# A prototype-matching block with a quantised FFN: VectorE's short operations rewritten, and the call orders of four engines changed

## The reference, cut to what matters

```python
xn = (x - mean_c(x)) / sqrt(var_c(x) + 1e-6)           # over the 96 channels
y[v, j] = <xn_j, w_mask_v> / (|xn_j| |w_mask_v|)       # cosine with 512 prototypes
v, j = argmax(y); top = y[v, j]; sims = y[v, :]        # of all 512 x 9
mix = concat(xn_j * top + w_mask_v * (1 - top), sims)  # 96 + 9
vcs = tanh(W_i2 leaky_relu(W_i1 mix + b, 0.2) + b)
h2  = W_l2 relu(W_l1 vcs + b) + b                      # 288 = 32 x 9
t   = x + fold(W_conv h2)                              # residual
n   = (t - mean_c(t)) / sqrt(var_c(t) + 1e-5)
out = t + q(W2 q(relu(q(W1 q(n)) + b1)) + b2)          # q: fp8 e5m2 / fp16 grid
```

## Time and profile before

| | |
|---|---|
| median of 3 runs | 2237.98 us (2236.76 to 2238.84) |
| the profiled execution | 2232.82 us |
| its span, first to last instruction | 2231.0 us |
| mean granted TensorE clock | 0.975 |

### The profile page before, as it was taken

One profiled execution on the slowest core, in us unless ns is written; L12 is line 12 of the kernel. 1 busy time (PEld: TensorE's weight loads), 2 busy tenths in 40 slices (PEclk: granted clock), 3 DMA queues, 4 the chain that ended last, 5 costly groups with the idle time before them and its releaser, 6 DMA issues.

```text
span 2231.0 us, 47761 instructions
## 1 busy us (share of the span) xinstructions
PE 2007.8 (90%) x13105; PEld 1485.3 (67%) x13105; DVE 2111.6 (95%) x7422; ACT 1834.2 (82%) x5381; POOL 1548.6 (69%) x1041
## 2 busy tenths in 40 slices
PE   5889999999999999999999999999999999999865
PEld 4566766667666676666766667676666766767653
DVE  7889999999999999999999999999999999999952
ACT  1158888888888888888888888888888888888886
POOL 2467677777767767677676777767777677777742
PEclk9899999999999999999999999999999999999975
DMA  3212323222232232322323232232322323223101
GB/s 98 76 58 81 99 82 107 81 91 96 87 101 82 90 97 85 103 81 91 97 84 104 82 97 92 89 98 82 105 83 89 99 81 99 89 89 98 42 37 48
DMA packets 65481, 193.34 MB, mean 87 GB/s; under 512 B 13688, under 2 KB 15938, under 8 KB 65218
## 3 DMA queue, kind: packets, MB, share of 16 engines
q1 hardware_dynamic: 52866, 170.80, 23.8%
q0 software_dynamic: 10240, 18.89, 2.9%
q10 hardware_dynamic: 2112, 0.60, 0.1%
HBM read 133.23 MB, written 57.02 MB: 85 GB/s over the span
## 4 chain that ended last, share of the span: by engine, by line
DVE 42%; PE 23%; POOL 22%; issue 11%; ACT 2%; POOLq 1%; DMA 0%; ACTq 0%; DVEq 0%
DVE best_y L1031 14%; POOL xl L400 6%; DVE stats L1040 5%; PE bank L701 5%; POOL prod L379 5%; POOL o_pm L391 4%; POOL t_dev L368 4%; DVE h L1048 4%; PE y_ps L646 3%; POOL tq L356 3%; PE y_ps L648 3%; PE y_ps L647 3%; DVE top_v L1070 2%; DVE w_index L1077 2%; DVE t_pm L1056 2%
## 5 line engine op out<-in xcount | busy, mean ns | idle before, releaser
L1031 DVE TENSOR_REDUCE best_y<-y_ps 128x2 f32<-128x1024 f32 (+1 forms) x640 | 698.0, 1107 | 17.5 <-PE y_ps L648 14.6
L463 ACT CAST y<-bank 128x384 f16<-128x384 f32 x1152 | 554.1, 481 | 72.8 <-PE bank L671 68.4
L646 PE MATMUL y_ps<-proto_hi,xh 96*128 96x512 f32 x1152 | 573.4, 498 | 43.6 <-DVE best_y L1031 16.1
L356 POOL TENSOR_TENSOR tq<-t_dev,ra 128x864 fp8e5<-128x864 f32 x128 | 209.4, 1636 | 537.8 <-DVE ra L1012 537.8
L671 PE MATMUL bank<-tqt,f_w 96*128 96x384 f16 x1152 | 392.6, 341 | 141.6 <-ACT y L463 110.4
L472 ACT ACTIVATE h<-h 128x1152 fp8e5<-128x1152 f16 x384 | 448.8, 1169 | 68.3 <-DVE h L1048 68.2
L647 PE MATMUL y_ps<-proto_lo,xh 96*128 96x512 f32 x1152 | 460.4, 400 | 0.0
L648 PE MATMUL y_ps<-proto_hi,xl 96*128 96x512 f32 x1152 | 459.6, 399 | 0.0
L671 PEld LDWEIGHTS bank<-tqt,f_w 96*128 96x128 f16 x1152 | 111.6, 97 | 382.2 <-ACT y L463 266.6
L400 POOL TENSOR_TENSOR xl<-xc,xh 96x1152 fp32r<-96x1152 f32 x128 | 336.9, 2632 | 26.5 <-ACT xh L533 15.8
L1048 DVE TENSOR_SCALAR h<-y,f_b 128x1152 f16<-128x1152 f16 x384 | 306.9, 801 | 22.5 <-ACT y L463 22.5
(11 more groups left out here) (133 smaller groups left out, 4115.9 us busy)
## 6 DMA issues: line engine op xcount, KB each, us to landing
xc<-x_cm SPq DMA_DIRECT2D x128, 432.0 KB, 3.9
xp<-x_pm SPq DMA_DIRECT2D x128, 432.0 KB, 4.6
out<-o_pm SPq DMA_DIRECT2D x128, 432.0 KB, 2.4
xsel<-x_pm,x_index POOLq DMA_INDIRECT x128, 2.5
wsel<-proto_rows,w_index POOLq DMA_INDIRECT x128, 4.7
proto_rows<-proto SPq DMA_DIRECT2D x1, 384.0 KB, 2.7
proto<-w_mask SPq DMA_DIRECT2D x1, 192.0 KB, 3.7
f_f<-w_1t ACTq DMA_DIRECT2D x1, 144.0 KB
```

Of the source, the lines that this page charges most:

```text
L463: act.copy(y16[:, q, r, 0:TOK], bank[0][:, 0:TOK]).then_inc(s_y16, 1)
L646: pe.matmul(y, hi, proto_hi[:], start=True, stop=False)
L1031: dve.tensor_reduce(best_y[t % 2][:, j0:j1], y_ps[n % 2][:, 0:j1 - j0, :], AX_X, ALU.max).then_inc(s_yd, 1)
```

## The change

The inverse root becomes a quartic in `w = guess * guess * value`, seven operations instead of nine, the guess in one operation. Its values are now 36 per patch instead of 27, since the norm of `x`, the sum of squares of `t`, and both variances lie in one row (`va`, now double-buffered; ACT writes its sums into it). One `variances` replaces `x_var` and `t_var`, with a row `eps` of constants. `x_sum` replaces `x_two` and `x_mean`. Product and maximum of `cos` and `best_cos` become one `tensor_tensor_reduce`; the other seven entries of `top` are filled with 3e38 once. `next_rows` goes: `row_base` holds the bases of all tiles from the start. The semaphore `s_va` goes. And the lists of DVE, PE, ACT and POOL are put in another order.

```diff
@@ -32,6 +32,8 @@
 NC = 9
 TOK = JP // 3
 
+QUARTIC = (-0.6773455142974854, 0.9603146314620972, -3.18097186088562, 2.961082935333252)
+
...
-        m_two = sb("m_two", [P, J])
-        mean2_x = [sb(f"mean2_x{b}", [P, J]) for b in range(RING)]
+        x_sums = [sb(f"x_sums{b}", [P, J, 2]) for b in range(RING)]
-        sq_t = sb("sq_t", [P, J])
-        va = sb("va", [P, 3 * J])
-        ra = [sb(f"ra{b}", [P, 3 * J]) for b in range(RING)]
+        va = [sb(f"va{b}", [P, 4 * J]) for b in range(2)]
+        ra = [sb(f"ra{b}", [P, 4 * J]) for b in range(RING)]
+        eps = sb("eps", [P, 2 * J])
...
@@ -423,9 +426,9 @@
             def slot(s):
                 lock(s)
                 t_norm(s)
+                product(s)
+                t_center(s)
                 gather_x(s)
-                t_center(s)
-                product(s)
                 output(s)
                 low_x(s)
...
                         if j == 0:
                             run.wait(s_dev, t + 1)
-                            run.wait(s_va, t)
+                            run.wait(s_rt, s - MATCH)
                             run.apart()
                         ins = act.activation(sq_junk[:, j * C:(j + 1) * C], t_dev[t % 2][:, j * C:(j + 1) * C],
-                                             ACT.Square, accum_out=sq_t[:, j:j + 1])
+                                             ACT.Square, accum_out=va[(s + 1) % 2][:, J + j:J + j + 1])
...
@@ -561,30 +564,30 @@
 
             def slot(s):
                 ffn1_out(s, 0)
-                high(s)
                 vcs_out(s)
                 ffn1_out(s, 1)
                 hidden8(s, FFN2, 1)
+                high(s)
                 ffn1_out(s, 2)
+                hidden8(s, FFN2, 2)
                 xnt_out(s)
+                ffn1_out(s, 3)
+                layer1_out(s)
                 mix_out(s)
-                layer1_out(s)
-                ffn1_out(s, 3)
-                hidden8(s, FFN2, 2)
+                weighted(s)
+                turned(s, 0)
+                ffn1_out(s, 4)
+                turned(s, 1)
                 hidden1_out(s)
-                ffn1_out(s, 4)
-                turned(s, 0)
                 ffn1_out(s, 5)
-                weighted(s)
+                hidden8(s, FFN, 0)
                 squares(s, range(0, 2))
-                turned(s, 1)
                 ffn1_out(s, 6)
-                hidden8(s, FFN, 0)
                 squares(s, range(2, 4))
+                ffn2_out(s, 0)
+                ffn1_out(s, 7)
+                ffn2_out(s, 1)
                 squares(s, range(4, 7))
-                ffn1_out(s, 7)
-                ffn2_out(s, 0)
-                ffn2_out(s, 1)
                 ffn1_out(s, 8)
...
@@ -754,36 +757,36 @@
                     last.then_inc(s_i1, 1)
 
             def slot(s):
+                hidden2(s)
+                ffn1(s, 0)
                 match(s, 0)
-                ffn1(s, 0)
-                hidden2(s)
                 ffn1(s, 1)
                 conv(s, 0)
+                ffn1(s, 2)
                 match(s, 1)
-                ffn1(s, 2)
-                turn_x(s)
                 conv(s, 1)
                 match(s, 2)
-                turn_mix(s)
+                turn_x(s)
+                match(s, 3)
                 ffn1(s, 3)
                 layer1(s)
+                turn_mix(s)
+                turn(s, 0)
+                ffn1(s, 4)
+                turn(s, 1)
                 hidden1(s)
-                match(s, 3)
                 match(s, 4)
-                ffn1(s, 4)
                 match(s, 5)
-                turn(s, 0)
                 ffn1(s, 5)
-                turn(s, 1)
+                ffn2(s, 0)
                 pick(s)
+                ffn1(s, 6)
+                ffn2(s, 1)
                 match(s, 6)
-                ffn1(s, 6)
-                ffn2(s, 0)
+                ffn1(s, 7)
                 match(s, 7)
-                ffn2(s, 1)
+                ffn1(s, 8)
                 match(s, 8)
-                ffn1(s, 7)
-                ffn1(s, 8)
 
...
@@ -874,14 +881,8 @@
                     t = s - SELECT
                     run.wait(s_rt, t + 1)
                     run.wait(s_yd, NG * (t + 1))
-                    steps.done("cos", dve.tensor_tensor(cosj[:], best_y[t % 2][:], ra[t % RING][:, 0:J], ALU.mult))
-
-            def best_cos(s):
-                if run.live(s, SELECT):
-                    t = s - SELECT
-                    steps.need("cos")
-                    run.apart()
-                    steps.done("top", dve.max(top[t % 4][:], cosj[:]))
+                    steps.done("top", dve.tensor_tensor_reduce(cosj[:], best_y[t % 2][:], ra[t % RING][:, 0:J], 1.0, -3e38,
+                                                               ALU.mult, ALU.max, top[t % 4][:, 0:1]))
 
             def best_j(s):
                 if run.live(s, SELECT):
...
+                    dve.tensor_tensor(x_index[t % 2][:], top_j[:, 0:1], row_base[:, t:t + 1], ALU.add).then_inc(s_xi, 1)
 
...
-            def x_two(s):
-                if run.live(s, MATCH):
-                    st = stats[(s - MATCH) % 2]
-                    steps.done("two", dve.tensor_tensor(m_two[:], st[:, :, 2], st[:, :, 5], ALU.add))
-
-            def x_mean(s):
+            def x_sum(s):
                 if run.live(s, MATCH):
                     t = s - MATCH
                     st = stats[t % 2]
-                    steps.done("mean", dve.tensor_tensor(mean2_x[t % RING][:], st[:, :, 1], st[:, :, 4], ALU.add))
+                    steps.need("x")
+                    steps.done("sum", dve.tensor_tensor(x_sums[t % RING][:], st[:, :, 1:3], st[:, :, 4:6], ALU.add))
 
...
+            def variances(s):
+
+                if run.live(s, MATCH) or run.live(s, NORM):
+                    if run.live(s, MATCH):
+                        steps.need("norm")
+                    if run.live(s, NORM):
+                        run.wait(s_sq, s - NORM + 1)
+                        run.apart()
+                    steps.done("va", dve.scalar_tensor_tensor(va[s % 2][:, 2 * J:], va[s % 2][:, 0:2 * J], 1.0 / C, eps[:],
+                                                              ALU.mult, ALU.add))
...
 
                 if run.live(s, MATCH) or run.live(s, NORM):
-                    r = ra[(s - MATCH) % RING]
+                    v, r = va[s % 2], ra[(s - MATCH) % RING]
                     if k == 0:
-                        if run.live(s, MATCH):
-                            steps.need("va")
-                        if run.live(s, NORM):
-                            run.wait(s_va, s - NORM + 1)
-                        steps.done("r", dve.tensor_scalar(r_t[:].bitcast(I32), va[:].bitcast(I32), 1, None,
-                                                          ALU.logical_shift_right))
-                        return
-                    steps.need("r")
-                    if k == 8:
-                        dve.scalar_tensor_tensor(r[:], r_u[:], 5.0, r1[:], ALU.add, ALU.mult).then_inc(s_rt, 1)
-                        return
-                    steps.done("r", [
-                        lambda: dve.tensor_scalar(r[:].bitcast(I32), r_t[:].bitcast(I32), -1.0, float(0x5F3759DF),
-                                                  ALU.mult, ALU.add),
-                        lambda: dve.tensor_tensor(r_t[:], r[:], r[:], ALU.mult),
-                        lambda: dve.scalar_tensor_tensor(r_u[:], r_t[:], -0.5 * 0.375, va[:], ALU.mult, ALU.mult),
-                        lambda: dve.scalar_tensor_tensor(r1[:], r_u[:], 1.5 * 0.375, r[:], ALU.add, ALU.mult),
-                        lambda: dve.tensor_tensor(r_t[:], r1[:], r1[:], ALU.mult),
-                        lambda: dve.scalar_tensor_tensor(r_v[:], r_t[:], 1 / 0.375 ** 2, va[:], ALU.mult, ALU.mult),
-                        lambda: dve.scalar_tensor_tensor(r_u[:], r_v[:], -10.0 / 3, r_v[:], ALU.add, ALU.mult),
-                    ][k - 1]())
+                        steps.need("va")
+                        steps.done("guess", dve.tensor_scalar(r_t[:].bitcast(I32), v[:].bitcast(I32), -0.5, float(0x5F1A56BF),
+                                                              ALU.mult, ALU.add))
+                    if k == 1:
+                        steps.need("guess")
+                        steps.done("square", dve.tensor_tensor(r_u[:], r_t[:], r_t[:], ALU.mult))
+                    if k == 2:
+                        steps.need("square")
+                        steps.done("w", dve.tensor_tensor(r_v[:], r_u[:], v[:], ALU.mult))
+                    if k == 3:
+                        steps.need("w")
+                        steps.done("first", dve.scalar_tensor_tensor(r_u[:], r_v[:], QUARTIC[0], r_v[:], ALU.add, ALU.mult))
+                    if k == 4:
+                        steps.done("second", dve.scalar_tensor_tensor(r1[:], r_v[:], QUARTIC[2], r_v[:], ALU.add, ALU.mult))
+                    if k == 5:
+                        steps.need("first")
```

(60 more changed lines are left out.)

56 lines of the change are left out of this document (25 added, 31 removed).

## The result

The changed kernel takes **2091.57 us** (median of 4 runs, 2089.68 to 2093.68) where the kernel before takes 2238.41 on the same chip: a ratio of 0.9344, with a 95% interval of 0.9328 to 0.9360. The profiled execution took 2092.94 with a span of 2090.8; before the span was 2231.0, so the traces have 140.2 us to explain.

What follows compares the result with a forecast made beforehand. DVE's instruction list was taken to bound the kernel: 118 slots x 0.78 = 92 us, fill 4 saved, setup 1 lost, drain nothing, giving 2138 profiled and 2143 us median; own range 2128 to 2160, widened to 2126 to 2186.

Steps and rivals of the forecast that it cites:

- DVE bounds the steady part: Steady slots: DVE, busy 99.0%, sets the pace with its own instruction list; slot falls from 16.38 to 15.60 us.
- Rival 1: Steady slots: PE sets the pace because waits for ACT's copies stay; slot 15.8 to 16.0, time 2181 us; chance 0.16.
- The terms of the short group: DVE's short instructions per slot: fusion, sums, merged variances, gaps filled, shorter root; together 0.74 us saved.
- The term of 0.10 for the wait of `best_j`: DVE: `best_j` no longer waits for the maximum, standing nine calls later; with two waits of 0.03, 0.10 us saved.
- The large instructions only move: DVE's long instructions cost the same wherever they stand, such as `ffn_bias(FFN2, 2)` at 0.72 us; no gain counted.
- the 0.1 of holes: DVE ahead of `y_max(1)`: about 0.1 us of small idle gaps per slot goes, as more work stands in front.
- For the drain ... nothing by my choice: End of the kernel: the old trace cannot price the new orders, so 0 us taken, range -8 to +8.
- 4 saved: Fill of ten slots at the start, partly DVE's and partly PE's at lower clock: 4 us saved, range 0 to 8.
- The cover: Whether PE, POOL and ACT keep up with DVE's shorter slot: they do, PE with about 0.3 us to spare.
- The walk: New PE order with old durations, counted from `low_part`: `turn(0)` at 6.15 us, `pick` results ready 11.4, DVE needs them 11.35.
- Rival 2: ACT delays `bank[0]` copies behind `hidden8`, PE waits up to 1.17 us each; slot 17.0, time 2309 us; chance 0.07.
- Rival 3: DVE's `remainder`, outside the lock, waits up to 1.7 us for POOL's `product`; time 2345 us; chance 0.02.

## Why the prediction was right, and where it fell short

The mechanism was right in the steady part: DVE's list sets the pace, and a shorter list shortens every slot. The time missed the range by three terms of the sum that were too small: the fill (by 18 us), the steady part (by 17) and the drain (by 10).

- **DVE bounds the steady part: right**, more so than forecast, at 99.7% with no waits. Rival 1 (PE paces) did not come: PE is busy 14.92 of 15.44.
- **The terms of the short group: right in sum to 0.06** (0.80 for 0.74). The fused pair costs 0.09, since its accumulator read starts with the next instruction (958.21 twice), 0.03 less than I took from `junk_mean`; and the old pair cost 0.20 per slot on average, where I took 0.16. (The term of 0.10 for the wait of `best_j` was added up wrongly: its own three waits, 0.08 and twice 0.03, make 0.14.) The seven root operations take 1.25 from the first (960.50) to `residual(0)` (961.75), for 1.17 and 0.09 in the forecast. `one_hot`, `index` and the two selections lie in gaps. `x_sum` to `x_norm` is 0.19, forecast 0.20. `remainder` costs 0.06, forecast 0.08.
- **"The large instructions only move": this step failed in the steady part, by 0.10 per slot.** I priced an instruction the same wherever it stands, and of the 0.1 of holes that I named I put 0.04 into the sum. The kernel with old operations and new orders has `h` at 2.14, as short as after, so the 0.10 of holes went with the orders. With 0.06 of the short group this makes the 0.16 per slot: 109.2 us over 116 slots where 92 were forecast.
- **"For the drain ... nothing by my choice" and "4 saved" for the fill: these two terms failed by 10 and by 18 us**, 28 of the 45 by which the traces differ from the forecast. (The medians differ by 6.6 us more than the profiled executions, mostly because the one of the kernel before, 2232.82, was 5.6 faster than its median.) I priced the fill as DVE's work and the drain at nothing, and both are PE's and ACT's order. The pair of old lists has 208.9 and 128.2 with all the new DVE work. In the fill of the kernel before, DVE waits for scores long before the pace is reached:

```profile
87.45 1.23 DVE L1031 TENSOR_REDUCE best_y<-y_ps 128x2 f32<-128x1024 f32 x1 [2.41 <-PE y_ps L648]
...
132.78 1.23 DVE L1031 TENSOR_REDUCE best_y<-y_ps 128x2 f32<-128x1024 f32 x1 [2.19 <-PE y_ps L648]
```

Between 76 and 150 us the kernel before has seven such waits, 8.0 us in all; the one after has one, of 1.43. PE was busy 18.16 of 24 us there at a granted clock of 0.79, and is now busy 21.29 at 0.90; the windows of the kernel before, for the same stretch of the fill and for 30 us from about the last `cosj`, as 1977 to 2007 is above:

```profile
76.00:100.00 24.00, 18.16 (x69) 13.13 (x68) 20.82 (x90) 4.87 (x11) 9.15 (x6) 0.79 0.30 85
...
2106.20:2136.20 30.00, 21.30 (x150) 15.17 (x150) 19.25 (x66) 26.40 (x84) 17.84 (x13) 0.89 0.11 38
```

In the drain the clock is the same to 0.02 (0.89 and 0.87). ACT is busy 28.05 of 30 us instead of 26.40 and PE 23.79 instead of 21.30: more of their work is done per us. Which call of the two lists carries it stays open, since the lists can't be parted without a clash; I did not try single calls.
- **The cover: right in outcome, and thin, as I called it.** The walk put `turn(0)` 6.15 after `low_part`, and `pick`'s results at 11.4 against DVE's 11.35. The rows of PE:

```profile
963.82 0.45 PE L663 MATMUL bank<-ident,tq 128*96 128x128 f16 x5 [0.44 <-POOL tq L359]
...
967.40 1.09 PE L740 MATMUL bank<-proto_t,xnt 96*128 96x512 f32 x2
```

`turn(0)` starts at 963.82, 6.06 behind `low_part` (957.76); `pick` ends at 968.49, 10.73; DVE comes at 968.95, 11.19. The slack is 0.46, where the walk had 0.05 too little; PE's part was 0.6 shorter than walked. (Its own terms up to `turn(0)` add up to 6.04 and not 6.15; between POOL's end at 963.67 and `turn(0)` the trace has 0.15.) What the walk did not do is ask what happens if the slack goes: the nine-step kernel loses 1.63 per slot where the roots themselves are 0.45. Nor did it price a call put where its partner does not expect it: `ffn_bias` alone, moved, is 3.5 per slot.
- **Rival 2 (ACT in the way) is real but needs an unmatched list**: 20.48 per slot with ACT's old one, where PE waits 2.4 per slot for the copies of `bank[0]`. In the pair as written PE has no such wait left.
- **Rival 3 (the instruction outside the lock) was priced by the wrong kind.** `remainder` took 0.14 beside `product`, as these rows of POOL with the DVE row at 963.99 show; `h` at 965.18 took its usual 0.80 beside it.

```profile
962.03 1.64 POOL L359 TENSOR_TENSOR tq<-t_dev,ra 128x864 fp8e5<-128x864 f32 x1 [2.99 <-DVE ra L1018]
963.63 2.02 POOL L382 TENSOR_TENSOR prod<-xp,wsel 128x864 f32<-128x864 f32 x1
```

Both read one SBUF tensor. `zb` on POOL held instructions that read two. The Trainium skill says this in "SBUF — State Buffer", section "SBUF: two separate sides": a VectorE instruction with two SBUF inputs and a POOL instruction that reads SBUF lock each other out for a whole instruction. The trace agrees, 1689 for 151 ns; my sentence that the trace does not bear the rule out held for one-input instructions alone. The changed kernel has a trace of it too, worth nothing in the total: `m_dif`, with two SBUF inputs, took 0.42 to 0.46 us instead of 0.16 in seven of the eight slots in which it ran beside `h1l` on POOL, as here.

```profile
895.70 0.68 POOL L412 TENSOR_TENSOR h1l<-h1f,h1h 113x128 fp32r<-113x128 f32 x1
...
895.96 0.45 DVE L929 TENSOR_TENSOR m_dif<-stats 128x9 f32<-128x9 f32 x1
```

## What to carry to other kernels

Orders written out for several engines are one object: a list must be costed with its partners, since here PE's or ACT's put back alone cost 5 to 6 us per slot and the pair 0.9. Before a shorter DVE list is priced, ask for each result who waits for it and by how much it is early, in the ramps too, where another engine may set the pace. And a DVE instruction with two SBUF inputs, however small, is to be priced at the whole of the POOL operation that it may meet: `va` took 2.4 to 2.5 us beside one of 1.84.

## What the runs showed of the hardware that was not expected

- A nine-element addition on DVE took 2.46 us beside a POOL operation of 1.84 and ended with it, though its own record starts 0.57 earlier than POOL's (307.55 and 308.12). Here, then, the starts of the records do not say which of the two went first.
- The accumulator read of a fused operation starts 0.09 after its operation and at the same time as the next instruction: in the changed kernel it costs between 0.00 and 0.03 from start to start.
- PE's granted clock was lower in the runs in which PE idled, over whole runs: 0.98 in the changed kernel, 0.95 with the nine-step root, 0.89 with `ffn_bias` moved back, 0.87 with PE's old list. It does not follow the idle time in step: with ACT's old list PE is as idle as with PE's (from 300 to 1800 us busy 1181.7 and 1204.3 us) at 0.94 and 0.88. In the changed kernel PE is busy 1449.0 us there at 1.00, which is 14.9 per slot; the 1204.3 us with PE's old list are 17.5 per slot. So part of the large losses of the clashing lists is matmuls at the lower of the two levels (1.2 and 2.4 GHz), and the waits alone do not add up to them.
